# Best-32 attention: a quarter of the marks on GpSimd, flag sums before new scores, quad copies first

## The reference

```
Q = (x_text @ Wq).reshape(B, T, 4, 32); K = (x_vision @ Wk).reshape(B, G, 4, 32)    # G = 4096 keys
scores = einsum('bthd,bghd->bhtg', Q, K) / sqrt(32)
topv, topi = top_k(scores, 32)
probs = softmax(topv)                      # only the 32 best keys of a row count
attn_mean = (probs put back at topi, zero elsewhere).mean(axis=heads)
c_t = einsum('btg,bgd->btd', attn_mean, x_vision @ Wv)      # then FiLM, S4D convolution, feed-forward
```

## Time and profile before

| | us |
|---|---|
| median of three runs | 1052.7 (1051.69 to 1053.14) |
| profiled execution | 1046.04 |
| its span | 1044.7 |
| best-32 stage in it | about 633 to 913 |

### The profile page before, as it was taken

One profiled execution on the slowest core, in us unless ns is written; L12 is line 12 of the kernel. 1 busy time (PEld: TensorE's weight loads), 2 busy tenths in 40 slices (PEclk: granted clock), 3 DMA queues, 4 the chain that ended last, 5 costly groups with the idle time before them and its releaser, 6 DMA issues. The chain is left out here.

```text
span 1044.7 us, 21000 instructions
## 1 busy us (share of the span) xinstructions
PE 916.4 (88%) x7731; PEld 572.7 (55%) x7731; DVE 796.7 (76%) x1671; ACT 668.9 (64%) x1077; POOL 342.1 (33%) x367
## 2 busy tenths in 40 slices
PE   6998989999999999996889977867887778898777
PEld 5887744444444444443648864723464556635545
DVE  4766879999999999932457987998877776379267
ACT  4654448888888888884445435179999999401222
POOL 2332268889950000000122531007373643000021
PEclk9999989999999999997799997666889999998979
DMA  7879763333333333201312219120354225780000
GB/s 207 290 253 307 253 198 81 81 85 82 84 81 86 85 85 80 68 2 21 104 46 86 83 38 245 27 66 1 98 157 128 61 61 168 241 208 15 1 1 21
DMA packets 99353, 111.87 MB, mean 107 GB/s; under 512 B 26674, under 2 KB 75746, under 8 KB 99250
## 3 DMA queue, kind: packets, MB, share of 16 engines
q1 hardware_dynamic: 98770, 110.19, 36.4%
q10 hardware_dynamic: 480, 0.33, 0.1%
HBM read 80.95 MB, written 29.43 MB: 106 GB/s over the span
## 5 line engine op out<-in xcount | busy, mean ns | idle before, releaser
L1041 ACT ACTIVATE pT<-bank 128x512 f32<-128x512 f32 x512 | 278.4, 597 | 54.5 <-PE bank L956 33.8
L1064 DVE TENSOR_REDUCE rmax<-bank 128x2 f32<-128x1024 f32 x240 | 290.5, 1224 | 8.6 <-PE bank L916 6.9
L971 PE MATMUL bank<-pT,V 128*17 128x256 f32 x2048 | 161.9, 388 | 4.2 <-ACT oT L1047 4.1
L1948 PE MATMUL bank<-K1s,qs 97*128 97x512 f32 x256 | 113.9, 549 | 34.2 <-ACT work L2072 13.8
L956 PEld LDWEIGHTS bank<-qs,ks 49*128 49x128 f32 x960 | 72.0, 185 | 98.9 <-ACT pT L1041 90.0
L956 PE MATMUL bank<-qs,ks 49*128 49x256 f32 x960 | 120.9, 329 | 1.8 <-ACT pT L1041 0.2
L2237 POOL TENSOR_TENSOR total<-total,work 128x1024 f32<-128x1024 f32 x40 | 94.8, 2378 | 33.8 <-ACT work L2072 33.0
L916 PE MATMUL bank<-ks,qs 49*128 49x512 f32 x480 | 97.3, 401 | 2.0 <-DVE rmax L1064 2.0
L1948 PEld LDWEIGHTS bank<-K1s,qs 97*128 97x128 f32 x256 | 53.7, 221 | 51.7 <-issue 36.3
L2132 DVE MAX8 cand<-work 128x8 f32<-128x128 f32 x384 | 76.5, 276 | 0.0
L971 PEld LDWEIGHTS bank<-pT,V 128*17 128x17 f32 x2048 | 34.5, 95 | 67.1 <-ACT pT L1041 50.7
(11 more groups left out here) (477 smaller groups left out, 1856.5 us busy)
## 6 DMA issues: line engine op xcount, KB each, us to landing
k_parts_d<-kparts SPq DMA_DIRECT2D x48, 512.0 KB, 4.0
ks<-k_parts_d SPq DMA_DIRECT2D x360, 64.0 KB, 2.2
K1s<-k_parts_d SPq DMA_DIRECT2D x96, 128.0 KB
cn<-in_ctx SPq DMA_DIRECT2D x32, 384.0 KB, 3.7
cx<-in_ctx SPq DMA_DIRECT2D x16, 384.0 KB, 4.3
w<-in_L_ffn_w SPq DMA_DIRECT2D x32, 128.0 KB, 2.8
w2e<-in_L_ffn_w SPq DMA_DIRECT2D x16, 128.0 KB, 2.4
W<-in_L_xattn_W SPq DMA_DIRECT2D x2, 1024.0 KB, 7.1
```

Of the source, the lines that this page charges most:

```text
L971: t = pe.matmul(bank[32 * c:32 * c + VW, 7, a * S:(a + 1) * S], V[:, b * NCH + 4 * g + c, h, :], pT[:, (at + 2 * (c // 2) + a) % 8, c % 2 ...
L1041: p_made.up(act.activation(pT[:, at % 8, :], bank[:, 4 + (at + 1) % 3, :], ACT.Exp))
L1064: max_read.up(dve.tensor_reduce(rmax[p % 2][:, :, qt, c], bank[:, b0:b0 + 2, :], AX.X, ALU.max))
L1948: m = pe.matmul(bank[:, b0 + c, :], qs1[0:NROW1, b * H1 + h, q], K1s[h][0:NROW1, keys], start=True, stop=(what == "new"))
```

## The change

The third quarter and the first two of `below` stay with ScalarE, the last goes to GpSimd: one `tensor_scalar` with is_lt against a per-row edge and is_equal with a second per-row number gives ones for what lies below. `settle` writes the edge (two values in the exact path). The weight matrix `minus` is -2^60 times the identity instead of -1 times it, and STEEP is 2^36 instead of 2^66. GpSimd does the mark of tile t + 1 between its third and fourth addition of tile t, or alone where it adds nothing. `sum_over` is issued between the "cut" and the "new" piece of a quarter. `copy_quad` stands first in its step on ScalarE.

```diff
-    NEX = 9
+    NEX = 11
-    LOW, FAR = -3e38, 1e30
-    STEEP = 2.0 ** 66
+    LOW, LOW_EDGE, FAR = -3e38, -2e38, 2.0 ** 60
+    STEEP, DEEP = 2.0 ** 36, 2.0 ** 60
...
-                pe.wait_ge(*below_made.at(4 * t + k + 1))
+                if k < 3:
+                    pe.wait_ge(*below_made.at(3 * t + k + 1))
+                else:
+                    pe.wait_ge(*last_below.at(t + 1))
...
+            sums_now = s > 0 and k == (s < NTL)
             for what in pieces_of(s, k):
+                if sums_now and what[0] == "new":
+                    if s == 1:
+                        pe.wait_ge(*q1_low.at(H1))
+                    sum_over(s - 1)
+                    sums_now = False
                 piece(*what)
-            if s and k == (s < NTL):
-                if s == 1:
-                    pe.wait_ge(*q1_low.at(H1))
+            if sums_now:
                 sum_over(s - 1)
...
             for k in range(4):
+                if 4 * s + k in quads:
+                    copy_quad(*quads[4 * s + k])
                 for what, t, piece in pieces_of(s, k):
...
-                    minus_made.up(act.activation(minus[:, :], identb[:, :], ACT.Identity, scale=-1.0))
+                    minus_made.up(act.activation(minus[:, :], identb[:, :], ACT.Identity, scale=-DEEP))
...
-                        mark_below(s - 1, k - 1, 2)
+                        mark_below(s - 1, k - 1, 2 if k == 1 else 1)
...
-                    mark_below(s - 1, k, 1)
+                    if k < 3:
+                        mark_below(s - 1, k, 1)
...
-                if 4 * s + k in quads:
-                    copy_quad(*quads[4 * s + k])
...
-            dve.wait_ge(*steep_usual.at(max(t + 1, 2)))
+            dve.wait_ge(*steep_usual.at(2 * max(t + 1, 2)))
...
+                exact.up(dve.memset(edge[:, 0, j:j + 1], LOW_EDGE))
+                exact.up(dve.memset(edge[:, 1, j:j + 1], 0.0))
...
-                dve.tensor_scalar(steep_thr[:, j:j + 1], top[j][:, KTOP - 1:KTOP], STEEP, None, ALU.mult).then_inc(exact.sem, NEX)
+                dve.tensor_scalar(edge[:, 0, j:j + 1], top[j][:, KTOP - 1:KTOP], 1.0, None, ALU.mult).then_inc(exact.sem, NEX - 1)
+                dve.tensor_scalar(steep_thr[:, j:j + 1], top[j][:, KTOP - 1:KTOP], STEEP, None, ALU.mult).then_inc(exact.sem, 1)
...
         for j in range(2):
+            steep_usual.up(pool.memset(edge[:, 1, j:j + 1], 1.0))
             steep_usual.up(pool.memset(steep[:, j:j + 1], -STEEP))
-        for t in range(LATE):
-
-            pool.wait_ge(*below_made.at(4 * (t + 1)))
-            steep_usual.up(pool.memset(steep[:, t % 2:t % 2 + 1], -STEEP))
-            if t % H1 == 0:
+
+        def mark_last(t):
+            j, part = t % 2, slice(3 * 1024, 4 * 1024)
+            pool.wait_ge(*picked.at(t + 1))
+            if t:
+                pool.wait_ge(*s_made.at(nth["cut", t - 1, 3] + 1))
+            last_below.up(pool.tensor_scalar(below[:, part], home(t)[:, part], edge[:, 0, j:j + 1], edge[:, 1, j:j + 1],
+                                             ALU.is_lt, ALU.is_equal))
+
+        mark_last(0)
+        for t in range(NTL):
+            pool.wait_ge(*below_made.at(3 * (t + 1)))
+            if t < LATE:
+                pool.wait_ge(*last_below.at(t + 1))
+                steep_usual.up(pool.memset(edge[:, 1, t % 2:t % 2 + 1], 1.0))
+                steep_usual.up(pool.memset(steep[:, t % 2:t % 2 + 1], -STEEP))
+            if t % H1 == 0 or t >= LATE:
+                if t < LAST:
+                    mark_last(t + 1)
                 continue
             acc = total[t // H1 % 3]
             for k in range(4):
+                if k == MARK_AT:
+                    mark_last(t + 1)
```

More of the change, by code:

```diff
@@ L1809, in build @@
     over_i = [sb(f"over_i{j}", [1, 1], I32) for j in range(2)]
-    ntop, steep_thr = sb("ntop", [P, 2]), sb("steep_thr", [P, 2])
+    ntop, steep_thr, edge = sb("ntop", [P, 2]), sb("steep_thr", [P, 2]), sb("edge", [P, 2, 2])
     etop = sb("etop", [P, KTOP])
@@ L1829, in build @@
         "lsum_made", "ebias_made", "added", "below_made", "steep_usual", "e_summed"))
-    late_added = flag("late_added")
+    late_added, last_below = flag("late_added"), flag("last_below")
     total_turned, aT_made, c0_made, c0_copied, tm_in, tmask_made, c0_turned, c0T_made = (flag(n) for n in (
@@ L1867, in build @@
             quads[4 * s + k] = (grp, n)
-    K_BANK, K_TURN = 7, 5
+    K_BANK, K_TURN, MARK_AT = 7, 5, 3
     def best_sync():
```

## The result

The median is 1040.86 us (1038.37 to 1043.53, 4 runs) against 1052.2 of the kernel before on the same chip, a ratio of 0.9895, 95% interval 0.9861 to 0.9928. So it is faster, by 11.3 us where 16.1 were forecast. Run again with more repetitions, the changed kernel had 1044.48 against 1050.72: 0.9941 (0.9916 to 0.9967), some 6 us. The profiled execution took 1042.73 us for a span of 1041.2, 3.5 less than the span of before, and not the 16.1 of the sum.

A forecast was written before the change was run, and what follows sets the result against it. ScalarE was taken to set the pace in the best-32 stage. Savings of 2.2, 11.5, 1.7, 0.5 and 1.7 us made -17.6; +1.5 for clock dips gave -16.1, so 1036.6 us from 1052.7, range 1031 to 1046.

The forecast's parts named there:

- The pace of ScalarE: Best-32 stage: 0.87 us leaves each ScalarE round; quad rounds take 12.44 us, rounds without quads 11.82, paced by VectorE.
- the third of the idle time kept: Quad rounds: clock dips on TensorE leave a third of 4.5 us of ScalarE stalls, adding 1.5 us.
- The size of GpSimd's pass: GpSimd's marking of a tile's last quarter takes 1.1 us, with 1.0 and 2.4 as ends.
- The tail: From mark 15 (ScalarE's on tile 15) to the last group's first copy: 0.5 and 1.7 us less.
- 12 us of room: GpSimd's pass on the next tile has a round, 12 us, for 1.1 us of work before its piece is due.
- this kind of wait for step 15: In step 15 early quad copies wait for transposes issued in the same step: 1.4 us for k = 1, 1.0 for k = 3.
- the rival in which the new order stalls ScalarE: Each of 24 early copies waits 0.7 us for transposes, 16.8 us go, time stays about 1053; chance 0.04.
- the sign named for it: Quad copies on ScalarE (L2082) showing idle time outside step 15 would show the forecast wrong.
- the GpSimd rival: GpSimd sets the pace from a pass of 4.9 us; at 8 us about 1078; sign: TensorE waits for its marks; chance 0.06.
- The chain of eight copies behind it moves by that: After the last group's first copy, its chain of eight copies only shifts, 1.7 us earlier.
- The early sums: Flag sums ahead of new scores: VectorE's 19.0 us of waiting falls to nearly nothing, but was mostly off the path.
- The rival with TensorE as the pace: TensorE's low clock half the time keeps quad rounds at 13.88 us; about 1047 us; chance 0.17.

The follow-up runs named there:

- The kernel whose steps 15 and 16 are the same: The changed kernel without the early flag sums, run twice: 1042.14 us (ratio 0.9933), then 1040.45 us (0.992).
- VectorE's marks at 11.90: The changed kernel with step 16's quad copies last in their quarter and all four quarters of tile 15 marked by VectorE: 1029.96 us, ratio 0.9821.

## Why the prediction was right in sign and too large

*The pace of ScalarE: right.* 0.87 us leaves each round, and the quad copies lose their idle time. Six of the eight quad rounds measure 12.25 or 12.26, forecast 12.44; the other two are 13.23 and 13.12. The whole is 99.88, forecast 99.5, or 101.0 with the third of the idle time kept. The first two rounds without quads are 11.63 and 11.64, forecast 11.82, and VectorE sets their pace, as forecast: each mark in them begins 0.09 us after VectorE has made `ntop`, its last instruction in `settle`. VectorE's row and ScalarE's:

```profile
709.07 0.15 DVE L2189 TENSOR_SCALAR ntop<-top 128x1 f32<-128x1 f32 x1
```

```profile
708.25 1.02 ACT L2048 COPY total<-bank 128x1024 f32<-128x1024 f32 x1
709.31 2.09 ACT L2070 ACTIVATE below<-work,steep_thr,steep 128x2048 bf16<-128x2048 f32 x1
```

ScalarE's copy has a slot of 0.89 elsewhere (700.98 to 701.87), so some 0.17 us of waiting lie before this mark where 0.3 were expected. What is smaller than forecast is VectorE's own round, and by ScalarE alone it would be about 11.5. The third such round is 12.01; VectorE was later there by 0.4 us, after idle time for which its trace names no releaser. The two long quad rounds each hold an idle time of 0.55 before an exponential, behind a weighing of 2.2 to 2.3 us and a turning of 1.06 on TensorE, which take 1.46 and 0.60 at the high clock.

*The size of GpSimd's pass: wrong.* It measures 3.78 us, outside the bounds of 1.0 to 2.4. Both rows that I bounded it with are arithmetic, and neither has a compare. GpSimd is busy 12.00 of 12 us now, and 145.2 instead of 86.7 in the long stretch. In the rounds this cost nothing that shows, as the pass has a round of room and every fourth round is without additions; doubling it shows how far it could have gone. The Trainium skill's rule (GPSIMD Engine Reference, section 7), about 2 cycles per element for such a body, gave an estimate of 1.7 us: it had the direction right and less than half of the size.

*The tail: the step that failed.* "The first copy of the last group ... 894.1 ... -1.7", with one copy done before mark 15, -2.2. It measures +8.1. These 10.3 us are most of the 11.6 between -16.1 and the -4.5 of stage start to end. The forecast let the copy wait "only for VectorE's addition"; but in ScalarE's queue it still stands behind the exponential of tile 15's last quarter, and in the trace it follows that exponential directly (888.86 and 889.88). So whatever makes this exponential late is paid in full. Three things were missed there. First, the copy of step 16 was put first and charged nothing. The transposes that it waits for stand on TensorE behind the cut piece of tile 15's first quarter, and that needs ScalarE's mark at 866.55, which comes right before the copy. ScalarE waits for a chain that it has just started itself. I worked out this kind of wait for step 15 (1.4 and 1.0, measured 1.30 and 0.98) and not for step 16. Second, the pass on tile 15 can't begin until the cut piece of tile 14 has been made, and in step 16 there is no round of room behind it; the cover of "12 us of room" ends with the loop. Third, the clock was low: 0.79, 0.78 and 0.64 of full speed instead of 1.00, in the windows above. The kernel whose steps 15 and 16 are the same and whose clock is 1.00 there has a tail shorter by 5.6. Undone alone, the order returned 6.9 us and the last pass 4.7, but both of these runs had the better clock too, so neither figure is the price of the edit: the kernel with early order, last pass and full clock, at 17.77, is shorter than the one that has only the last pass undone, at 18.67. In kernels whose clock is 1.00 for the first 12 us of the tail, order and pass cost 1.4 and 0.3 (17.77 to 16.41 to 16.10). It is the rival in which the new order stalls ScalarE, at one place instead of 24, and the sign named for it came: a copy with idle time outside step 15. The sign of the GpSimd rival came as well, TensorE waiting 3.12 us for a mark, at the last tile alone.

What of the 16.10 against the forecast 13.0 remains was not taken apart in full. The wait before the last exponential is 2.21 us there and was 1.30 before, with a clock of 0.50 in those 4 us against 0.91; and VectorE's marks at 11.90 show that the mark and piece chain of tile 15 is in it.

*Behind the tail: +2.5 us, forecast 0.* "The chain of eight copies behind it moves by that" doesn't hold either. From the first to the eighth copy it took 14.50 us for 13.14, with a clock of 0.78 for 0.87, and the rest to the end 136.82 for 135.69, where the same 492 matmul records took 113.92 us for 112.39. All kernels with any of the edits took 0.7 to 2.9 us more here than the kernel before, that with the sums alone too, so it is no matter of GpSimd. Why the clock comes out lower there stays open.

*The early sums: no gain, as forecast, but for another reason.* VectorE's wait for the sum fell from 19.0 to 2.8 us, as forecast, but this edit isn't what did it: with the other two edits alone the wait is 4.0. Left out beside early copies, the early sums change nothing in the quad rounds (99.38). Without early copies they cost 8 us. I had not priced the edit by itself: it is the order of copies that makes it harmless.

*The median.* The profiled execution was to take 1029.9 us and took 1042.73, 12.8 more. Of these, 11.6 lie between the stage's start and the end, and 1.0 ahead of it. The median missed by 4.3 only, 1040.86 for 1036.6, because the 6.7 us by which the median of before lies above its profiled execution, and which I took over, didn't come: after, it lies 1.9 below. Two errors offset each other there, and that the median came so near is luck.

The rival with TensorE as the pace didn't come: its clock in the quad rounds rose from 0.91 to 0.97 over 745 to 845 us. With step 16 alone in the old order it was 0.90 though, and marks 5 to 13 took 102.5 instead of 99.9, while nothing of their order had changed; the two kernels that give the last mark back to ScalarE took 102.5 as well, with 0.91 and 0.90. Why the clock takes one of two courses there stays open.

## What to carry to other kernels

Price an edit at the last step of a loop by itself: the slack that hides it in every round is the next round, and the last has none. An instruction moved to the head of an in-order queue is free only if what it waits for doesn't hang on something queued in front of it on the same engine a moment before. Before work goes to GpSimd, measure the very operation: arithmetic and compares of one shape are a factor of three apart there.

## What was not expected of the hardware

GpSimd's `tensor_scalar` over 128x1024 takes 1.05 to 1.20 us with multiply and add, 2.84 with one compare alone and 3.6 to 3.8 with two compares, with a compare and a multiply or with subtract and minimum; VectorE takes 0.69 to 0.81 for all of these.

VectorE's mark at 865.51 took 2.86 us beside GpSimd's addition from 865.38 to 867.82, and 0.80 to 0.88 otherwise. The Trainium skill (SBUF — State Buffer, "Who interferes with whom") says that `tensor_scalar` in a two-port mode and a GpSimd instruction exclude each other, and the trace agrees here. Beside GpSimd's compare pass it doesn't: that pass ran from 861.63 to 865.41, and within it VectorE's first mark took 0.88 us, as by itself, and its addition at 864.37 took 1.23, as by itself too. So what GpSimd is doing matters, and not only that it is busy. The rule was weighed in the prediction for the one-element `edge` alone, where nothing is seen (0.15).

The same instructions in the same order took 23.33 or 17.77 us, each in two profiled executions within 0.02, with TensorE's clock low in the first 12 us of the one and full in those of the other. A stretch that repeats exactly is no proof that its order of work alone sets its time.
